# First cross attention of a Perceiver kernel: a tile is projected one round later, and GpSimd takes over three steps of the normalising

## What is computed

```python
    x = x + _L0_xattn_ref(_layernorm(x, axis=-1), ctx_768, ...)

def _L0_xattn_ref(x, y, wq, bq, wk, bk, wv, bv, wo, bo):
        q = (x @ wq + bq).reshape(B, SQ, N_HEADS, D_HEAD)
        k = (y @ wk + bk).reshape(B, SKV, N_HEADS, D_HEAD)
        v = (y @ wv + bv).reshape(B, SKV, N_HEADS, D_HEAD)
        scores = jnp.einsum('bqhd,bkhd->bhqk', q, k) / jnp.sqrt(jnp.asarray(D_HEAD, x.dtype))
        attn = jax.nn.softmax(scores, axis=-1)
        out = jnp.einsum('bhqk,bkhd->bqhd', attn, v).reshape(B, SQ, D_EMBED)
        return out @ wo + bo
```

## Time and profile before

| what | value |
|---|---|
| runs shown | 2078.38, 2077.34 and 2070.31 us |
| median | 2077.34 us |
| profiled execution | 2077.73 us |
| its span, first to last instruction | 2075.9 us |
| busy share of the span | PE 90%, PEld 76%, DVE 63%, ACT 45%, POOL 37% |
| mean granted TensorE clock | 0.951 of full speed |

### The profile page before, as it was taken

How to read it: one execution, slowest core, us unless ns; L and a number is a source line. 1 busy time by engine, 2 the same in 40 slices (tenths; PEclk the granted TensorE clock), 3 DMA queues, 4 the chain that set the end, 5 groups by cost and what they waited for, 6 DMA issues and landing times.

```text
span 2075.9 us, 44097 instructions
## 1 busy us (share of the span) xinstructions
PE 1869.8 (90%) x17906; PEld 1575.8 (76%) x17906; DVE 1302.7 (63%) x2795; ACT 940.2 (45%) x2016; POOL 775.4 (37%) x826
## 2 busy tenths in 40 slices
PE   5999999999999598696999999999999989779994
PEld 4778778787787477585999999999999856546662
DVE  4778787787877765543766767666676536532222
ACT  4666666666665433343444444444444334112221
POOL 4656565565564522205333333333333023130002
PEclk9999999999999798896999999999999999789997
DMA  6121112111200200103223222232222070311002
GB/s 199 40 59 34 34 39 61 34 34 34 65 2 2 93 1 1 49 14 100 56 57 106 62 56 56 56 99 69 56 57 56 1 281 1 122 59 31 31 29 71
DMA packets 55656, 119.81 MB, mean 58 GB/s; under 512 B 4432, under 2 KB 41888, under 8 KB 53920
## 3 DMA queue, kind: packets, MB, share of 16 engines
q1 hardware_dynamic: 53920, 112.80, 18.3%
q0 software_dynamic: 1536, 4.20, 0.6%
HBM read 107.80 MB, written 9.18 MB: 56 GB/s over the span
## 4 chain that ended last, share of the span: by engine, by line
PE 72%; DVE 11%; ACT 7%; issue 5%; DMA 2%; POOL 1%; SPq 0%; POOLq 0%; DVEq 0%; ACTq 0%
PE ps L163 7%; PE ps L104 7%; PE ps L2136 6%; PE ps L480 5%; PE ps L462 5%; PE ps L439 4%; PE ps L1344 4%; PE ps L2160 3%; PE ps L1345 3%; PE ps L456 2%; DMA wsb<-in_ctxT 2%; PE ps L1330 2%; PE ps L1329 2%; DVE arena L1437 2%; PE ps L1333 2%
## 5 line engine op out<-in xcount | busy, mean ns | idle before, releaser
L539 DVE TENSOR_REDUCE arena<-ps 128x1 f32<-128x400 f32 (+1 forms) x512 | 257.6, 566 | 119.2 <-PE ps L439 119.1
L665 ACT ACTIVATE arena<-ps 128x384 f32<-128x384 f32 (+1 forms) x512 | 223.3, 524 | 126.7 <-PE ps L462 126.7
L737 POOL TENSOR_TENSOR arena<-arena 128x512 f32<-128x512 f32 (+1 forms) x160 | 209.8, 1312 | 174.0 <-ACT arena L665 95.2
L1344 PE MATMUL ps<-arenaR 128*128 128x386 f32 x768 | 246.4, 356 | 1.1 <-DVE arenaR L1431 1.1
L1530 ACT CAST arenaR<-ps 128x512 fp32r<-128x512 f32 (+1 forms) x256 | 116.6, 507 | 226.1 <-PE ps L163 226.0
L1345 PE MATMUL ps<-arenaR 128*128 128x256 f32 x768 | 215.5, 281 | 0.0
L1573 POOL TENSOR_TENSOR arenaR<-h,arenaR 128x400 fp32r<-128x400 f32 (+1 forms) x60 | 57.8, 964 | 378.6 <-ACT arenaR L1515 378.6
L1431 DVE TENSOR_TENSOR arenaR<-ps,arenaR 128x512 fp32r<-128x512 f32 (+1 forms) x256 | 138.8, 584 | 25.8 <-ACT arenaR L1530 25.6
L1413 DVE TENSOR_TENSOR arenaR<-wsb,arenaR 64x400 fp32r<-64x400 f32 x64 | 66.0, 1036 | 136.7 <-ACT arenaR L1516 136.7
L1344 PEld LDWEIGHTS ps<-arenaR 128*128 128x128 f32 x768 | 145.1, 189 | 1.4 <-DVE arenaR L1431 1.3
L1345 PEld LDWEIGHTS ps<-arenaR 128*128 128x128 f32 x768 | 146.0, 190 | 0.0
(11 more groups left out here) (318 smaller groups left out, 4658.9 us busy)
## 6 DMA issues: line engine op xcount, KB each, us to landing
wsb<-in_ctx SPq DMA_DIRECT2D x16, 1152.0 KB
arena<-in_ctxT SPq DMA_DIRECT2D x16, 800.5 KB, 5.1
arena<-in_ctxT SPq DMA_DIRECT2D x32, 400.2 KB, 7.3
wsb<-in_ctxT SPq DMA_DIRECT2D x32, 400.2 KB, 7.3
gu<-in_m_gu SPq DMA_DIRECT2D x8, 1536.0 KB, 21.1
h<-in_ctxT SPq DMA_DIRECT2D x15, 800.5 KB, 4.9
dn<-in_m_dn SPq DMA_DIRECT2D x8, 768.0 KB, 9.2
xs_rows<-zeros SPq DMA_DIRECT2D x1, 2944.0 KB, 16.1
```

The lines of the kernel that those rows point to most:

```text
L539: e.tensor_reduce(mx4[n % 2][:, u, i:i + 1], ps[:, at("look", n, i, u), 0:400 + (i == 3)], AX.X, ALU.max).then_inc(c.maxed.at((n, i, u)), 1)
L665: e.activation(v[:, u, 0:128 * GN[s]], ps[:, at("st", n, s, u), 0:128 * GN[s]], ACT.Exp).then_inc(c.exp_a.at((x0, n, s, u)), 1)
L737: e.tensor_tensor(acc_p[0:k], acc_p[0:k], v[0:k, :, 128 * t:128 * t + 128], ALU.add).then_inc(added_p.at((n, s)), 1)
L1344: e.matmul(o, PTh[:, t, :], v[:, t, 0:386], start=(t == 0), stop=False)
```

## The change

- `projects` names the odd round 8t + 9 for tiles 0 to 6; tile 7 keeps round 64.
- GpSimd gets `add_both`: one addition of `acc_d` to `acc_p` behind step 3 of each group, and L489's eight matmuls become four (L487) on the merged `acc_p`, which wait for it.
- `normalise` is split. VectorE keeps the reciprocal in the even round (`invert`). The sum of the values' halves and the product with the reciprocal go to GpSimd (`scale`), in the same even round behind its additions and ahead of its split. The two picking steps stay on VectorE as `gather`, one round later, behind the second maxima of the odd round.
- Waits follow: VectorE's first addition of a group waits for the merge, and ScalarE's `take_sum` for `scaled` in place of `o_norm`.

```diff
-        return r // 8 - 1 if r % 8 == 0 and 1 <= r // 8 <= NT else None
+        return NT - 1 if r == LAST else (r - 9) // 8 if r >= 9 and r % 8 == 1 else None
...
             if half:
-                w.wait_ge(*added_d((n, 3)))
-                w.wait_ge(*added_p((n, 3)))
+                w.wait_ge(*added_p((n, "all")))
                 w.wait_ge(*padded("rows"))
-                for a, v in enumerate((acc_d, acc_p)):
-                    for u in range(4):
-                        o = e.matmul(ps[32 * u:32 * u + 32, bk, 128:256], ones, v[:, u, :], start=(a == 0), stop=(a == 1))
+                for u in range(4):
+                    o = e.matmul(ps[32 * u:32 * u + 32, bk, 128:256], ones, acc_p[:, u, :], start=True, stop=True)
...
             if s == 0:
                 if n:
-                    w.wait_ge(*totals(n - 1))
+                    w.wait_ge(*added_p((n - 1, "all")))
                 e.tensor_tensor(acc_d, v[:, :, 0:128], v[:, :, 128:256], ALU.add).then_inc(added_d.at((n, s)), 1)
...
-        def normalise(n):
+        def invert(n):
+            w.wait_ge(*c.o_out((x0, 2 * n + 1)))
+            if n:
+                w.wait_ge(*c.po(("scaled", n - 1)))
+            e.reciprocal(rS, vb[:, 128:256]).then_inc(c.dv.at(("inverted", n)), 1)
+
+        def gather(n):
+
             b, g = n // 2, n % 2
             q = slice(64 * (b % 2), 64 * (b % 2) + 64)
-            w.wait_ge(*c.o_out((x0, 2 * n + 1)))
-            e.reciprocal(rS, vb[:, 128:256]).then_inc(c.dv.at(), 1)
-            e.tensor_tensor(oS, va, vb[:, 0:128], ALU.add).then_inc(c.dv.at(), 1)
-            w.wait_ge(*c.dv.now())
-            e.tensor_tensor(oS, oS, rS, ALU.mult).then_inc(c.dv.at(), 1)
-            w.wait_ge(*c.dv.now())
+            w.wait_ge(*c.po(("scaled", n)))
             w.wait_ge(*c.in_const("small"))
...
             if r >= 2 and r % 2 == 0:
-                normalise(r // 2 - 1)
+                invert(r // 2 - 1)
+            if r >= 3 and r % 2:
+                gather((r - 3) // 2)
             for use in groups(r)[1:]:
                 add(*use)
+        gather(N - 1)
         project(projects(LAST))
...
             if n:
-                w.wait_ge(*c.o_norm((x0, n - 1)))
+                w.wait_ge(*c.po(("scaled", n - 1)))
             v = vb if r % 2 else va
...
+        def add_both(n):
+            w.wait_ge(*added_d((n, 3)))
+            w.wait_ge(*added_p((n, 3)))
+            e.tensor_tensor(acc_p, acc_p, acc_d, ALU.add).then_inc(added_p.at((n, "all")), 1)
+
+        def scale(n):
+
+            w.wait_ge(*c.o_out((x0, 2 * n + 1)))
+            if n:
+                w.wait_ge(*c.o_norm((x0, n - 1)))
+            e.tensor_tensor(oS, va, vb[:, 0:128], ALU.add).then_inc(c.po.at(), 1)
+            w.wait_ge(*c.po.now())
+            w.wait_ge(*c.dv(("inverted", n)))
+            e.tensor_tensor(oS, oS, rS, ALU.mult).then_inc(c.po.at(("scaled", n)), 1)
+
...
             for use in groups(r)[1:]:
                 add(*use)
+                if r % 2:
+                    add_both(r // 2)
+            if r >= 2 and r % 2 == 0:
+                scale(r // 2 - 1)
             if splits(r) is not None:
                 split(*splits(r))
```

## The result

| | before | after |
|---|---|---|
| median of the runs | 2077.33 us (2070.31 to 2078.38) | 2052.45 us (2048.74 to 2055.48) |
| profiled execution, its span | 2075.9 us | 2050.2 us |

The ratio is 0.9887, with a 95% interval from 0.9859 to 0.9914: 24.9 us faster. The same kernel, compared once more with the kernel before on another chip, gave 2046.42 against 2078.66 us, ratio 0.9846 (0.9824 to 0.9868), 32 us faster. The forecast was 2042.8 us, 34.9 us faster. The first result is inside the range of 2036 to 2062 and 9.7 us slower than the forecast.

What follows compares the result with a forecast made beforehand. The prediction took TensorE to pace the first cross attention. Its terms, -25.1 - 6.9 - 3.9 + 1.0 = -34.9 us against the profiled 2077.73 us, gave 2042.8 us, with a range of 2036 to 2062.

Steps and rivals of the forecast that it cites:

- What bounds the stage: First cross attention: TensorE paces it, matmul side busy 76.89 of 80 us, waiting only in a few places.
- Part 1: Projection one round later: seven projections cost 1.06 us each instead of 32.5 us in all, 25.1 us gained.
- Part 2: Sums' matmuls on TensorE: half go, 0.23 us per head group, 30 groups counted, 6.9 us gained.
- Part 3: GpSimd's merge before L487 in odd rounds: ends 0.8 us in time in a short round, costed at nothing.
- Rival A: Short odd rounds: the merge comes late 16 times, 8 to 15 us lost, time near 2055; chance 0.15.
- Part 4: Adding and scaling on GpSimd: VectorE is earlier in odd rounds, 21 bank waits go, 3.9 us gained.
- Part 5: End of the stage: exposed merge 1.61 and scaling 0.80 lose 2.4 us, less 1.4 gained: 1.0 us lost.
- The sum: Whole change: -25.1 - 6.9 - 3.9 + 1.0 = -34.9 us, giving 2042.8 us; this case's chance 0.72.
- The bound of 38 us: Largest gain of the forecast case: 25.1 + 7.4 + 3.9 + 1.4 = 38 us.
- Rival C: TensorE's waits for exponentials grow by what is taken out, so the gain does not arrive: 2072 us; chance 0.08.
- Rival B: GpSimd's odd-round queue becomes the pacer through 7.1 us of new holds per group: slower, 2088 us; chance 0.05.

Runs made afterwards that it cites:

- kernel 1: Kernel before with only the projection moved to the odd round, normalising whole on VectorE, two sums: 2054.49 against 2081.5 us, ratio 0.9886.
- kernel 3: Kernel before with projection moved and sums merged, normalising left whole on VectorE: 2048.74 against 2081.5 us, ratio 0.9851.
- Kernel 4: Full change without the merge, eight matmuls on two sums again: 2063.67 against 2081.5 us, ratio 0.9914.
- kernel 9: Full change with GpSimd's merge issued three times (sum, difference, sum): 2097.36 against 2079.15 us, ratio 1.0106.
- kernel 6: kernel 3 measured again, on the chip of the full change's second comparison: 2046.73 against 2078.66 us, ratio 0.9859.
- kernel 7: Full change with group 30's scaling before GpSimd's last addition of step 1 and the last group's sums unmerged: 2049.51 against 2078.66 us, ratio 0.986.
- 10: Full change with only the scaling of group 30 ahead of GpSimd's additions of step 1: one run of 2053.45 us.
- 11: Kernel 4 with VectorE's gather ahead of the second maxima: 2059.68 against 2079.15 us, ratio 0.991.
- 12: Full change with VectorE's gather ahead of the second maxima: 2051.31 against 2079.15 us, ratio 0.988.

## Why the prediction was right, and where it was not

- **What bounds the stage**: right. Taking TensorE's own stalls and passes out shortened the stage, and every experiment changed its length through what TensorE issued or waited for.
- **Part 1, 25.1 us**: right in mechanism; that the stage of kernel 1 gives the same tenth is luck. Its two assumptions held: no drop of the clock without the stall, and a bare pair near 18.71 us (18.80 in kernel 1: 139.86 - 121.06). But the lower clock was read from one projection and put at 9.5 us for seven; it fell behind five and cost 7.6, and the stall itself cost 17.0 and not the 15.6 of its rows. The steady rounds gained 25.5, and 0.5 lost at the end was in no part.
- **Part 2, 6.9 us**: right. On top of the projection the merge gained 6.8 us in the steady rounds (562.7 to 555.9, kernels 1 and 3) and lost 1.5 at the end. The 7.4 us of the merge alone hold 3 us of clock.
- **Part 3, hidden**: right, and as thin as said. The merge was taken to end 0.8 us in time and had 0.56. Rival A did not occur, but its trigger, the gather slowed by GpSimd, did: the gather was sized 0.35 us per step and its second took 1.2. What kept the cover was something I had not listed: the merge makes GpSimd wait for VectorE's addition, and the gather and that addition end in this pause (604.29 and 604.89, GpSimd idle from 604.20 to 604.97). Kernel 4, without the pause, has the gather at 2.0 us. The sign of rival A, L487 waiting for the merge, shows only in the last two groups, 2.1 and 2.3 us.
- **Part 4, 3.9 us for the bank waits**: mis-sized. The 21 waits did go, but kernel 3, which still has 5.1 us of them, loses only 2.0 us in the steady rounds (555.9 against 553.9). TensorE came to the keys earlier and waited there for exponentials: L390's waits for exponentials were 9.3 us in 14 cases in the kernel before, 9.9 in 15 in kernel 3, and are the 12.5 in 29 shown above. So 2.6 us of the 5.1 came back one step later; that this is one cause is read from the table of waits and not tested apart.
- **Part 5, 1.0 us lost**: mis-sized, 3.1 were lost. The merge was put at 1.6 and cost 1.5. The scaling was put at 0.8 us lost and 1.4 gained, because ScalarE's copy would wait less; the copy waited 3.4 us instead of 2.6, and the move cost 1.2 there. I had not counted that the scaling of group 30 is queued behind GpSimd's additions, and the last exponentials behind the copy. Repairing that order alone gave 2.1 us back, and with the last merge left out 3.6. The remaining 0.5 came with the projection.
- **The sum** for the stage was 34.9 us and came to 31.2: part 4 is 1.9 short and part 5 2.1, and parts 1 and 2 gave 0.3 more. The other 5.5 us of the first profile lie outside the stage (1.1 at the start, 4.4 behind), which the prediction took as constant. The timed runs gained 24.9 us in the first comparison and 32 in the second, so how near the forecast of 34.9 comes depends on the comparison. The bound of 38 us for the gain leaves out the 2.4 us that part 5 itself counts as lost; it only widens the range.
- **Rival C** fell: L480's waits are what they were (39.7 us before, 40.8 after, in 60 to 640 us). **Rival B** fell; kernel 9 holds the merge back 2.6 us more in every group, and GpSimd still does not set the pace.

## What to carry to other kernels

A stall of the pacing engine can cost more than its row of the table of waits: here 2.23 us in the row, 2.43 in the period, and 1.5 more in the five cases of seven in which the clock fell behind it. Read the period with and without the stall, and look at every case before multiplying one. When work moves between VectorE and GpSimd, look for the instructions with two SBUF inputs that will run beside each other: here the same move gained 0.8 us or cost 6.6, depending on whether GpSimd paused where VectorE's gather and addition stood. Where a new wait stands in an engine's queue, cost what is queued behind it, above all in the last rounds, where nothing covers it.

## What the runs showed that was not expected

The stages behind the changed one have the same instructions in every kernel, yet they took from 1362.4 to 1372.5 us. Two profiles, busy times from the last L104 to the end, first of kernel 6 (columns as above):

```profile
680.60:2043.00 1362.40, 1212.21 (x7382) 1033.77 (x7382) 754.60 (x1793) 498.51 (x1030) 360.35 (x466) 0.94 0.20 62
```

The same of kernel 7:

```profile
675.10:2047.50 1372.40, 1223.58 (x7382) 1043.15 (x7382) 754.39 (x1793) 498.00 (x1030) 359.81 (x466) 0.93 0.20 61
```

The same 7382 matmuls are busy 1212.21 and 1223.58 us, at a mean granted clock of 0.94 and 0.93. The busy times differ by 11.4 us and the stretches by 10.0. So some 10 us of such a comparison go with how much of the later stages runs at the lower of TensorE's two levels, which is as much as the difference between the forecast and the first result. Whether the end of the changed stage influences that is open: the eight profiles with the scaling on GpSimd (the full change twice, then 4, 7, 9, 10, 11 and 12) have 1370.3, 1369.3, 1370.3, 1372.4, 1367.0, 1372.5, 1370.3 and 1369.1 us, the six with all of the normalising on VectorE 1365.9 (before), 1366.6, 1369.6, 1365.9, 1362.4 and 1369.9. That is a tendency, not a cause shown.
